# Graph layers: expansion products as three bf16 pieces, and 0/1 matrices for two groups at a time

## What is computed

```python
def _spmm(row, col, vals, x):
    msg = vals[:, None] * x[col]
    return jax.ops.segment_sum(msg, row, num_segments=N)

def _layer(x_prev, row, col, vals, W_a, b_a, W_b, b_b):
    h = _spmm(row, col, vals, x_prev)
    z = (h + x_prev) @ W_a.T + b_a + h * x_prev @ W_b.T + b_b
    return jnp.where(z >= 0, z, NEG_SLOPE * z)

x = emb[x_ids]
x1 = _layer(x, row, col, vals, W1_1, b1_1, W1_2, b1_2)
x2 = _layer(x1, row, col, vals, W2_1, b2_1, W2_2, b2_2)
x3 = _layer(x2, row, col, vals, W3_1, b3_1, W3_2, b3_2)
return jnp.concatenate((x, x1, x2, x3), axis=1)
```

## Time and profile before

| | us |
|---|---|
| median of 3 runs | 9519.62 |
| lowest and highest | 9513.02, 9523.34 |
| profiled execution | 9515.19 |
| its span | 9513.4 |
| PE busy | 8731.2 (92%) |
| DVE busy | 7879.5 (83%) |
| ACT busy | 4383.1 (46%) |
| POOL busy | 5665.0 (60%) |

### The profile page before, as it was taken

How to read it: one execution, slowest core, us unless ns; L and a number is a source line. 1 busy time by engine, 2 the same in 40 slices (tenths; PEclk the granted TensorE clock), 3 DMA queues, 4 the chain that set the end, 5 groups by cost and what they waited for, 6 DMA issues and landing times.

```text
span 9513.4 us, 228026 instructions
## 1 busy us (share of the span) xinstructions
PE 8731.2 (92%) x69832; PEld 8032.5 (84%) x69833; DVE 7879.5 (83%) x11265; ACT 4383.1 (46%) x13668; POOL 5665.0 (60%) x3637
## 2 busy tenths in 40 slices
PE   7688886888888589999999999999999999999999
PEld 4577775577777479999999999999999999999999
DVE  7799998899999788877777788877777788877777
ACT  0578775177777346651111366631111566611112
POOL 8688886088888412228888422258888122278885
PEclk8788888888888689999999999999999999999999
DMA  2211111011111887778888677778889577788886
GB/s 80 37 6 6 6 6 19 7 6 6 6 6 6 27 180 280 280 278 284 287 286 286 196 279 281 280 279 287 286 286 286 192 279 282 281 281 286 287 286 205
DMA packets 1005649, 1718.92 MB, mean 181 GB/s; under 512 B 378356, under 2 KB 429624, under 8 KB 1004920
## 3 DMA queue, kind: packets, MB, share of 16 engines
q0 software_dynamic: 378656, 958.17, 33.8%
q1 hardware_dynamic: 499680, 751.43, 21.8%
q10 hardware_dynamic: 127224, 8.24, 3.0%
HBM read 961.68 MB, written 755.66 MB: 181 GB/s over the span
## 4 chain that ended last, share of the span: by engine, by line
PE 66%; DVE 20%; issue 9%; ACT 2%; DMA 1%; ACTq 1%; DVEq 0%; POOL 0%; SPq 0%; POOLq 0%
PE ps L951 34%; PE ps L942 24%; DVE place L1116 7%; DVE hT L1137 4%; DVE hT L1132 4%; PE ps L789 3%; DVE place L1119 2%; ACT work L713 1%; DVE hT L1260 1%; PE ps L839 1%; PE ps L959 1%; PE ps L979 1%; PE ps L980 1%; PE ps L813 1%; DVE place L1121 0%
## 5 line engine op out<-in xcount | busy, mean ns | idle before, releaser
L951 PE MATMUL ps<-work 128*128 128x125 f32 x28416 | 3281.8, 278 | 37.6 <-DVE work L1313 37.6
L951 PEld LDWEIGHTS ps<-work 128*128 128x128 f32 x28416 | 3240.6, 192 | 78.9 <-DVE work L1313 38.8
L547 POOL DMA_INDIRECT work<-messages,work x1776 | 2709.2, 1525 | 621.7 <-issue 621.7
L942 PE MATMUL ps<-xb,work 125*128 x21504 | 2452.2, 276 | 96.1 <-ACT work L713 77.8
L942 PEld LDWEIGHTS ps<-xb,work 125*128 125x128 f32 x21504 | 2421.0, 192 | 127.2 <-issue 127.2
L1313 DVE TENSOR_TENSOR work<-work,iota_p 128x1000 f32<-128x1000 f32 x1776 | 2120.8, 1194 | 35.0 <-ACT work L731 34.4
L713 ACT ACTIVATE work<-ps,work 128x128 f32<-128x128 f32 x5376 | 1537.1, 369 | 1109.5 <-PE ps L942 1109.5
L532 POOL PARTITION_BROADCAST work<-work x672 | 554.5, 827 | 2327.0 <-DMA work<-slot_cols 1283.4
L502 POOL DMA_INDIRECT sorted_edges<-stage,run_idx x798 | 1603.2, 2009 | 475.7 <-ACT stage L644 248.0
L731 ACT ACTIVATE work<-work 128x8 f32<-128x8 f32 x1776 | 534.4, 301 | 2668.3 <-DMA work<-messages,work 2668.3
L839 PEld LDWEIGHTS ps<-hT 128*128 128x128 f32 x12768 | 1621.3, 208 | 115.2 <-issue 90.4
(11 more groups left out here) (206 smaller groups left out, 4522.7 us busy)
## 6 DMA issues: line engine op xcount, KB each, us to landing
messages<-work SPq DMA_DIRECT2D x2688, 256.0 KB, 2.4
work<-messages,work POOLq DMA_INDIRECT x1776, 5.9
out_x<-xb SPq DMA_DIRECT2D x150, 125.0 KB
sorted_edges<-stage,run_idx POOLq DMA_INDIRECT x798, 3.3
work<-slot_cols SPq DMA_DIRECT2D x672, 2.0 KB
work<-lane_places SPq DMA_DIRECT2D x532, 5.2 KB, 2.1
out_x<-xb ACTq DMA_DIRECT2D x4, 1562.5 KB
sorted_edges<-hT SPq DMA_DIRECT2D x4, 908.0 KB
```

The costliest lines, as they stand in the source:

```text
L547: pool.indirect_dma_start(out=ck[:, n, :, :].rearrange("p h x -> p (h x)"), out_offset=None, in_=flat, in_offset=bass.IndirectOffsetOnAxis ...
L942: last = t.matmul(ps[:, n % PR, j * D:(j + 1) * D], col_hot[:, n % OHR, j * P:(j + 1) * P], x_flat[:, bass.ds(offs[n], D)], start=True, st ...
L951: last = t.matmul(part[n], ck[:, n, j // CH, j % CH * D:(j % CH + 1) * D], sel[:, n % SELB, j, :], start=j == 0, stop=j == CHB - 1)
```

## The change

**Three pieces.** At the start of each layer DVE splits x. The upper 16 bits of each f32, read in place as bf16 with a step of two (`x_high`), are the first piece. The rest, x minus that, is written as f32 into `hT` (`rest`, four operations of 3200 columns); its upper 16 bits, again read in place (`x_mid`), are the second. What then remains fits a bf16 exactly and is written packed into `work` (`x_low`, four more operations). PE waits for all of them (`pieces_ready`).

**Twelve bf16 matmuls a group instead of four f32 ones.** Each of the four products is summed in PSUM from three pieces.

**The 0/1 matrix** is bf16 and made for two groups by one operation of 1024 columns. It has the same four group slots, used as two pairs; one pair is made ahead. LEAD is gone. The messages stay as they are, the even groups on ACT and the odd ones on DVE.

**Zeroing.** `hT` is in use in stage A, so it is zeroed by one memset at the stage's end, after PE's last product.

`hT` grows to 12800 columns, `work` to 24080.

```diff
@@ PE @@
                 pe.wait_ge(xb_ready, la * DSTEPS + 1)
+                pe.wait_ge(pieces_ready, la * SPLITS + SPLITS)
...
                     for n in range(AU):
-                        pe.wait_ge(col_hot_ready, la * GROUPS + i * AU + (n + 1))
+                        if n % 2 == 0:
+                            pe.wait_ge(col_hot_ready, la * (GROUPS // 2) + i * (AU // 2) + (n // 2 + 1))
                         pe.wait_ge(msg_ready[n % 2], la * (GROUPS // 2) + i * (AU // 2) + (n // 2 + 1))
                         for j in range(CH):
-                            last = t.matmul(ps[:, n % PR, j * D:(j + 1) * D], col_hot[:, n % OHR, j * P:(j + 1) * P],
-                                            x_flat[:, bass.ds(offs[n], D)], start=True, stop=True)
+                            at = n % OHR * GE + j * P
+                            for k, piece in enumerate((x_high, x_mid, x_low)):
+                                last = t.matmul(ps[:, n % PR, j * D:(j + 1) * D], col_hot[:, at:at + P],
+                                                piece[:, bass.ds(offs[n], D)], start=k == 0, stop=k == 2)
                         last.then_inc(expanded, 1)
@@ DVE @@
+                dve.wait_ge(x0_got, NB * DMA)
+                dve.wait_ge(xb_ready, la * DSTEPS + 1)
+                W = HTW // SPLITS
+                for c in range(SPLITS):
+                    at = slice(c * W, (c + 1) * W)
+                    v.tensor_tensor(rest[:, at], x_flat[:, at], x_high[:, at], ALU.subtract).then_inc(rest_ready, 1)
+                for c in range(SPLITS):
+                    at = slice(c * W, (c + 1) * W)
+                    dve.wait_ge(rest_ready, la * SPLITS + (c + 1))
+                    v.tensor_tensor(x_low[:, at], rest[:, at], x_mid[:, at], ALU.subtract).then_inc(pieces_ready, 1)
...
-                    dve.wait_ge(expanded, la * GROUPS + i * AU + (n + 1))
-                    v.tensor_scalar(col_hot[:, n % OHR, :], col_row[0:BLK, n // BATCH, n % BATCH * GE:(n % BATCH + 1) * GE],
+                    dve.wait_ge(expanded, la * GROUPS + i * AU + (n + 2))
+                    v.tensor_scalar(col_hot[:, n % OHR * GE:(n % OHR + 2) * GE],
+                                    col_row[0:BLK, n // BATCH, n % BATCH * GE:(n % BATCH + 2) * GE],
                                     iota_c[0:BLK, :], None, ALU.is_equal).then_inc(col_hot_ready, 1)
...
-                    for n in range(AU):
-                        if n + LEAD < AU:
-                            make_hot(i, n + LEAD)
+                    for n in range(0, AU, 2):
+                        if n + 2 < AU:
+                            make_hot(i, n + 2)
                         elif not last_body:
-                            make_hot(i + 1, n + LEAD - AU)
-                        if n % 2:
-                            dve.wait_ge(expanded, la * GROUPS + i * AU + (OHR + n + 1))
-                            free_message(i, n, first)
-                            v.tensor_tensor(msg[:, n % MR, :].rearrange("p (j d) -> p j d", j=CH),
...
-                    v.tensor_scalar(hT[:, bass.ds(i * ZC, ZC)].rearrange("p (a z) -> p a z", a=2),
-                                    iota_p[:, 0:ZC // 2][:, None, :].to_broadcast([P, 2, ZC // 2]), 0.0, None, ALU.mult).then_inc(h_zeroed, 1)
-
-                for n in range(LEAD):
-                    make_hot(0, n)
+                            make_hot(i + 1, 0)
+                        dve.wait_ge(expanded, la * GROUPS + i * AU + (OHR + n + 2))
+                        free_message(i, n + 1, first)
+                        v.tensor_tensor(msg[:, (n + 1) % MR, :].rearrange("p (j d) -> p j d", j=CH),
...
+                make_hot(0, 0)
                 expand(0, True, False)
                 with dve.Fori(1, ABODIES - 1) as i:
                     expand(i, False, False)
                 expand(ABODIES - 1, False, True)
+                dve.wait_ge(expanded, la * GROUPS + (OHR + GROUPS))
+                v.memset(hT[:, 0:N], 0.0).then_inc(h_zeroed, 1)
...
-                dve.wait_ge(h_zeroed, la * ABODIES + ABODIES)
+                dve.wait_ge(h_zeroed, la + 1)
```

45 lines of the change are left out of this document (27 added, 18 removed).

## The result

The changed kernel takes 9794.37 us (median of four runs, 9792.57 to 9810.04) against 9521.48 for the kernel before: a ratio of 1.0291, 95% interval 1.0278 to 1.0304. The forecast was slower, 9555 us, with a range up to 9780. The sign was right; the size was 33 us where 273 were measured, and the time lies outside the range. The sign is owed to the head of each layer: stage A itself was forecast to gain 47 us and lost 177.

The account below looks back on a forecast made before the run. PE was taken to bind the kernel before, a PE-DVE loop stage A after. 9515 - 47 (stage A) + 81 (heads) + 3 (ends) = 9552, rounded to 9555 us with 4 us to the median; range 9420 to 9780.

Parts of the forecast that it names:

- What bounds, and the loop: Stage A: PE binds before; afterwards a PE-DVE loop of message, matrix and pair, two pairs in 3.30 us.
- The price of a matmul: Stage A: a bf16 matmul of 128 columns costs 0.056 us, the 24 of a pair 1.35 us.
- rival D: Slower: a matmul costs more, by 81 ns (9892 us) or double time for every-second-bf16 reads (about 10250); chance 0.06.
- Rival A: Faster: the loop is shorter than added up, 9422 us, or 9170 if PE never waited inside a body; chance 0.14.
- POOL's broadcast stretches some matrices ... 0.2: Stage A: matrices stretched by POOL's broadcasts, each now on the chain, add 0.2 us a body.
- Rival B: Port shared with POOL: from a matrix of 0.84 us a body takes more than before; priced at 1.28; chance 0.10.
- rival C: Slower: longer PE idle at a body's top lowers the clock (9755 to over 10500 us), or code loads (9800); chance 0.08.
- The top: Start of each stage A body: PE idle 1.7 us around the register load, bounds 1.1 to 1.9.
- Head and end: Split operations at the layers' heads cost 81 us together; the memset at stage A's ends 3 us (0 to 7).
- the case: The likeliest forecast, 9555 us, running from 9451 to 9675 by a body of 14.2 to 15.5 us; chance 0.62.

Follow-up runs that it names:

- e2: The changed kernel without POOL's broadcasts of the column numbers after the first body of each layer: 9554.75 us, ratio 1.0025 to the kernel before.
- e12: The changed kernel with the matrix of pair k+2 ahead of the message of pair k on DVE: 9401.7 us, ratio 0.9868 to the kernel before.
- e1: The changed kernel with eight group slots for four and three pairs made ahead for one: 9379.12 us, ratio 0.9842 to the kernel before.
- e11: The changed kernel with three pairs ahead, short register loads, 16 message slots and a quarter of the split on POOL: 9242.22 us, ratio 0.9702.
- e3: The changed kernel with two more unread f32 products of 448 columns behind each body's last pair: 9727.78 us, ratio 1.0211 to the kernel before.
- e4: The kernel before with only the split and the zeroing of the changed one, f32 products and single matrices kept: 9622.94 us, ratio 1.0098.
- e6: The changed kernel with the matrix made for one group at a time, three groups ahead: 9536.12 us, ratio 1.0021 to the kernel before.

## Why the prediction was wrong, step by step

**What bounds, and the loop: right.** PE bound the kernel before; the change put a loop of latencies in its place. The sum 0.29 + 0.61 + 0.75 + 0.20 + 1.45 = 3.30 for two pairs is met where nothing stretches a matrix: in e2 pair 4 starts 3.32 behind pair 2 and pair 6 another 3.40. The parts, medians and counted from the start of a pair's last product to the start of the last product two pairs on: 0.36, 0.61, 0.745, 0.16, 1.45. e12 shows that the 0.61 of the message in the middle decides it, and e1 that more slots do the same.

**The price of a matmul: right.** 57 ns, for packed and for every-second-element operands alike, against the forecast 0.056; rival D is out. Rival A is out too, as PE waits 2.0 us inside a body at full clock. The Trainium skill's figure for a stream of weight loads and matmuls, about 81 ns at N=128 ("TensorE: Matmul & The Clock Gate", section "Back-to-back issue gap"), does not hold for this one.

**"POOL's broadcast stretches some matrices ... 0.2": the first wrong step.** At full clock a body measured 15.60, not 14.8. e2 takes the broadcasts away and gets 14.67, which is the forecast without that term (14.6). So the term is 0.93 us a body, 156 us in all, where 0.2, 34 us, stood in the sum. The inputs were in front of me: a mean of 503 against a median of 479 ns, and a maximum of 1124, which is 16 x 0.024 = 0.38 us a body; I put half of it on the path. 197 of 2688 matrices were stretched then, 66 us in all. I did not ask how often a broadcast would meet a matrix once both hang on the same loop: 371 of 1344 are stretched now, 132 us in all. That is one half of the step that failed, and e2 shows it as 0.43 us a body of waits ahead of pairs, 72 us. The other half stood in no term: without the broadcasts the top is 0.31 us shorter, 52 us, and the rest is small gaps inside pairs. Why the top is shorter is not shown; the register load overlaps a broadcast in 159 of 168 bodies now and did so in 11 before. Rival B named this mechanism, the port shared with POOL, and said that from a matrix of 0.84 on a body takes more than before; the mean is 0.843. It had a chance of 0.10 and a matrix of 1.28 for its price.

The Trainium skill, "SBUF — State Buffer", section "🔬 SBUF: two separate sides", says that GpSimd and certain VectorE operations (those in a two-port fast mode, and two-input ones beside a GpSimd operation that reads SBUF) take a shared port pair in turn, whichever starts first, each for a whole instruction. The traces agree in kind: a matrix takes at most 749 ns without broadcasts and up to 1381 with them, and in e11 DVE's two-input operations take 15.6 us against 10.3, or POOL's wait 7.4 us.

**The clock: the second wrong step.** It was rival C, at 0.08, with "with 0.8 us of idle a body stage A kept 1.00, with 1.7 it may not" and a price of 1.2 us a body. The price was about right (16.70 - 15.60 = 1.10), and it fell due in every second body: 0.57 x 168 = 96 us. What failed is the weighing. The sum itself contained a top of 1.7 us and waits of 0.45 at every second pair, the very thing that the row on the clock spoke against the earlier trace rows, and I still took the clock as full in the likeliest case. e3 gives 67 us back by keeping PE busy; 27 of the 96 go to the filler's own delay (15.60 to 15.76).

**The top: a little low.** 1.7 forecast, 1.88 measured, 30 us; inside the bounds that I gave it (1.1 to 1.9). It is not a step beside the first: the top of e2 is 1.58.

**Head and end: right.** 81 forecast, 86 measured; 3 forecast (0 to 7), 8 measured, one over its bound, as the memset seems to take 13.0 us; e4 has 92 for both. Stage B got 6 us longer, for which I have no cause: the gathers and sums there are untouched (5.7 in e4, 3.4 in e2). The upper end of the case, 9675, counts the 4 us from execution to median, the lower, 9451, does not; nothing hangs on it. Of rival C the other half, code loads once a body, is out: the two instruction queues moved 44 and 45 packets before, 45 and 42 after (the earlier trace rows has the first queue only).

156 - 34 + 96 = 218 of the 225 us by which stage A was missed.

**What stays open.** The load of 16 registers at a body's top takes 1.10 us at least everywhere, but its median is 1.56 before, 1.78 after, 1.52 in e2 and 2.28 in e1. It has no obvious order with the transfers (share 0.74, 0.70, 0.77 and 0.84), nor with the broadcasts alone (148 of e1's 168 loads overlap one, 159 in the changed kernel). Why it grew was not tried. Nor is it shown what idle time brings the clock down: the changed kernel had 82 stretches at 1.2 GHz with a top of 1.88 and waits of 2.0 us, e2 one with 1.58 and 1.6, e1 25 with 2.2 and none, e6 75 with 2.2 and 0.5. e3 shows only that filling the top is enough.

## What to carry over

When a change makes the bound engine's work smaller, write down the loop that takes over, step by step from the release of a buffer to its next use, and look at what stands in it without need: here moving one matrix ahead of one message turned 2.9% slower into 1.3% faster, and splitting a register load in four took it to 3%. Every disturbance that had cover before (the broadcasts, the load, short idle times of PE) must then be priced at full length, and idle time on PE perhaps twice, since the clock may fall behind it: here the clock took 0.57 us a body beside 1.9 of idle at the top. The mean against the median of an operation shows such disturbances; whether they count is told by the slack behind it.

## What the runs showed of the hardware that I had not expected

More work on PE can make a kernel faster: 1.5 us of products that nobody reads, in a gap of 1.9, brought 67 us through the clock. A stretch of PE idle that had stayed harmless at 0.6 us a body turned costly at 1.9 with waits of 0.4 and more around it. At 2.2 without such waits (e1, e12) it brought 25 and 22 falls of the clock where there had been 82, but 75 in e6, whose waits sum to 0.5, so the length of the idle time alone does not tell. Stores of messages ran at 329 GB/s and a share of 0.89 with eight slots and at 332 and 0.90 with sixteen, while the time from issue to landing went from 4.9 to 10.9 us.
